# Four graph layers on one core: the leaky slope inside ScalarE's activation, another set-up, and new orders on every engine

## What is computed

```python
h = jnp.maximum(_layernorm(x, axis=-1), 0.0)
x = x + _L0_gnn_ref(h, ...)   # masked attention, 8 heads, projection, o + layernorm(o)
h = jnp.maximum(_layernorm(x, axis=-1), 0.0)
x = x + _L1_gnn_ref(h, ...)   # rel = adj.T * (h Wq.T)(h Wk.T).T / row norm; rel @ (h Wv.T)
h = jnp.maximum(_layernorm(x, axis=-1), 0.0)
x = x + _L2_gnn_ref(h, ...)   # graph attention, below
h = jnp.maximum(_layernorm(x, axis=-1), 0.0)
x = x + _L3_gnn_ref(h, ...)   # adj @ h @ weight + bias
```

```python
h = jnp.einsum('bnc,cf->bnf', x, W)
e = jax.nn.leaky_relu(s1[:, :, None] + s2[:, None, :], negative_slope=0.2)
e = e * mask[None, :, :]
att = jax.nn.softmax(e, axis=2)
return jax.nn.elu(jnp.einsum('bij,bjf->bif', att, h) + beta * h)
```

## Time and profile before

| | |
|---|---|
| median of 3 runs | 1473.15 us (1472.97 to 1476.63) |
| the profiled execution's own time | 1474.63 us |
| its span, first to last instruction | 1472.8 us |
| TensorE busy | 1438.2 us, 98% |
| VectorE busy | 1273.4 us, 86% |
| ScalarE busy | 1134.7 us, 77% |
| GpSimd busy | 748.4 us, 51% |

### The profile page before, as it was taken

One profiled execution on the slowest core, in us unless ns is written; L12 is line 12 of the kernel. 1 busy time (PEld: TensorE's weight loads), 2 busy tenths in 40 slices (PEclk: granted clock), 3 DMA queues, 4 the chain that ended last, 5 costly groups with the idle time before them and its releaser, 6 DMA issues.

```text
span 1472.8 us, 47814 instructions
## 1 busy us (share of the span) xinstructions
PE 1438.2 (98%) x16136; PEld 1370.3 (93%) x16136; DVE 1273.4 (86%) x5774; ACT 1134.7 (77%) x2884; POOL 748.4 (51%) x1107
## 2 busy tenths in 40 slices
PE   5999999999999999999999999999999999999996
PEld 5899999999999999999999999999999999999985
DVE  4889988988989889889889889889889889889885
ACT  4778878878877877877877778778778788788753
POOL 3455555555555555555555555555555555555452
PEclk9999999999999999999999999999999999999998
DMA  3000000100000000001001000000001001000000
GB/s 111 17 17 23 31 16 30 31 16 31 30 17 31 30 16 31 28 19 31 24 23 30 23 24 30 24 24 31 23 24 30 23 24 30 19 28 31 9 23 30
DMA packets 38113, 39.90 MB, mean 27 GB/s; under 512 B 2416, under 2 KB 37488, under 8 KB 37872
## 3 DMA queue, kind: packets, MB, share of 16 engines
q1 hardware_dynamic: 37872, 36.84, 7.9%
HBM read 20.05 MB, written 16.78 MB: 25 GB/s over the span
## 4 chain that ended last, share of the span: by engine, by line
PE 95%; DVE 1%; ACT 1%; issue 1%; POOL 0%; DMA 0%; SPq 0%; POOLq 0%; ACTq 0%; DVEq 0%
PE bank L314 34%; PE mid L314 15%; PE bank L349 6%; PE mid L358 5%; PE bank L520 5%; PE bank L370 4%; PE mid L458 4%; PE mid L374 4%; PE bank L330 4%; PE mid L488 4%; PE bank L417 4%; PE mid L330 2%; PE mid L349 2%; PE mid L493 1%; PE mid L527 1%
## 5 line engine op out<-in xcount | busy, mean ns | idle before, releaser
L546 ACT ACTIVATE probs<-masked,neg_max 128x128 f32<-128x128 f32 x1024 | 326.3, 395 | 6.3 <-DVE neg_max L716 6.3
L903 POOL TENSOR_TENSOR rstd<-var_eps,minus_half 128x2 f32<-128x2 f32 x320 | 240.9, 753 | 25.5
L716 DVE CUSTOM_DVE_ANT_0 masked<-mid,mask 128x128 f32<-128x128 f32 x1024 | 234.9, 286 | 6.9 <-issue 6.8
L915 POOL TENSOR_TENSOR xb<-x,b_proj_beta 128x512 f32<-128x512 f32 x64 | 81.9, 1279 | 233.9 <-DVE o_res L828 233.9
L901 POOL TENSOR_TENSOR var_eps<-mean_var,eps 128x2 f32<-128x2 f32 x320 | 63.5, 198 | 243.0 <-DVE mean_var L710 242.7
L706 DVE BATCH_NORM_STATS2 stats<-x 128x6 f32<-128x256 f32 x384 | 143.3, 415 | 0.1
L725 DVE TENSOR_SCALAR z<-x,mean_var,rstd 128x256 f32<-128x256 f32 x384 | 134.5, 405 | 7.1 <-POOL rstd L903 6.7
L946 POOL TENSOR_TENSOR h_t_lo<-h_t_full,h_t_hi 128x512 fp32r<-128x512 f32 x64 | 82.0, 1282 | 79.4 <-ACT h_t_hi L629 79.4
L349 PE MATMUL bank<-ident,probs 128*128 128x128 f32 x768 | 117.6, 276 | 4.9 <-ACT probs L546 4.9
L942 POOL TENSOR_TENSOR e_mask<-e_leaky,adj_sb 128x256 f32<-128x256 f32 x64 | 46.8, 731 | 116.2 <-DVE e_leaky L770 116.2
L370 PE MATMUL bank<-probs_t,v 128*32 128x128 f32 x2048 | 104.5, 276 | 0.3 <-issue 0.3
(11 more groups left out here) (156 smaller groups left out, 5725.8 us busy)
## 6 DMA issues: line engine op xcount, KB each, us to landing
x<-in_x SPq DMA_DIRECT2D x64, 256.0 KB, 2.7
out_x<-x SPq DMA_DIRECT2D x64, 256.0 KB, 2.1
w_qkv_sb<-in_w_qkv SPq DMA_DIRECT2D x1, 768.0 KB, 4.4
w_q_sb<-in_w_q SPq DMA_DIRECT2D x1, 256.0 KB, 4.4
w_k_sb<-in_w_k SPq DMA_DIRECT2D x1, 256.0 KB, 4.6
w_v_sb<-in_w_v_t SPq DMA_DIRECT2D x1, 256.0 KB, 5.8
w_proj_sb<-in_w_proj SPq DMA_DIRECT2D x1, 256.0 KB, 6.0
w_gat_x<-in_w_gat SPq DMA_DIRECT2D x1, 256.0 KB, 7.2
```

The costliest lines, as they stand in the source:

```text
L546: last = act.activation(probs[:, r, s], masked[:, r, s], ACT.Exp, scale=-1.0, bias=neg_max[:, r, s:s + 1])
L716: last = dve.tensor_tensor_reduce(out=masked[:, r, s], in0=mid[:, r, s * N:(s + 1) * N], in1=mask[:], scale=1.0, scalar=LARGE, op0=ALU.add ...
L903: pool.tensor_tensor(rstd[:, k], var_eps[:, k], minus_half[:], ALU.pow).then_inc(ln_rstd[k], 1)
```

## The change

**Leaky slope.** ScalarE reads s2 with the function Prelu and alpha 0.2 instead of Identity, with the same bias, and writes e_leaky itself. The tile e_sum, its semaphore and VectorE's pass are gone; GpSimd's e_mask now waits for two increments.

**Set-up.** w_qkv is rounded in three parts of 512 columns (q, k, v) on ScalarE and VectorE; both parts are issued ahead of VectorE's round 1, so the moments and z of pair 0 stand in front. TensorE's round 0 is only z0's transposes of pair 0; the fold stands behind them, ahead of round 1, and its two loads are issued behind CONSTS. ScalarE's copies of the fold come ahead of its round 2, its low part ahead of VectorE's round 3.

**Orders.** The order of the stages is another on all four engines, and so is the division into stages: k moves from on[0] to on[1] on TensorE, the transposes of probs 3 and the heads from on[1] to on[2], sum_sq to on[4], hw and s2 to on[5]. VectorE counts its stages one further (its last, x4, is on[8]), so `STREAMS` is 9; TensorE still uses on[0] to on[7]. The banks are assigned anew: z1, rel, y and the fold share bank 5, for instance. SP's loads and stores are counted to match.

```diff
-    STREAMS = 8
+    STREAMS = 9
...
             sp.dma_start(x0[:, 1], x_pairs[1]).then_inc(x_in[1], 16)
             for dst, src in CONSTS:
                 sp.dma_start(dst, src).then_inc(const_in, 16)
+            for dst, src in FOLD_CONSTS:
+                sp.dma_start(dst[:], src).then_inc(fold_in, 16)
...
+            def first_weights():
+                pe.wait_ge(fills_made, 3)
+                pe.wait_ge(w_lo_ready, 2)
...
-            run(pe, step, [(0, fold), (2, next_weights), (4, last_weights)])
+            run(pe, step, [(1, first_weights), (1, value_weights), (1, fold), (3, folded_weights),
+                          (2, next_weights), (5, last_weights)])
...
-            act.activation(w_qkv_p[0][:], w_qkv_sb[:], ACT.Copy).then_inc(w_hi_ready, 1)
+                for j in range(3):
+                    act.activation(w_qkv_p[0][:, :, j * D:(j + 1) * D], w_qkv_sb[:, :, j * D:(j + 1) * D], ACT.Copy)\
+                       .then_inc(w_hi_ready, 1)
...
-                    for b in range(2):
-                        act.activation(e_sum[:, b], s2_bank[:, b * N:(b + 1) * N], ACT.Identity, bias=hw[:, b, D:D + 1])\
-                           .then_inc(e_sum_ready, 1)
...
+                    for b in range(2):
+                        act.activation(e_leaky[:, b], s2_bank[:, b * N:(b + 1) * N], ACT.Prelu, bias=hw[:, b, D:D + 1], alpha=ALPHA)\
+                           .then_inc(e_leaky_ready, 1)
...
-            run(act, step, [(0, copy_fold)])
+            run(act, step, [(0, first_weights), (2, copy_fold)])
...
-                    dve.scalar_tensor_tensor(e_leaky[:], e_sum[:], ALPHA, e_sum[:], ALU.mult, ALU.max).then_inc(e_leaky_ready, 1)
...
-            run(dve, step, [(0, first_constants), (2, next_constants), (2, last_constants)])
+            run(dve, step, [(1, first_constants), (3, fold_low), (2, next_constants), (2, last_constants)])
...
-            run(pool, step, [(2, next_constants), (2, last_constants)])
+            run(pool, step, [(1, next_constants), (2, last_constants)])
```

## The result

The changed kernel took **1477.97 us** (median of 20 runs, 1474.88 to 1479.56), the kernel before beside it 1473.96 us (20 runs, 1472.97 to 1477.96): a ratio of **1.0021** (95% interval 1.0015 to 1.0028). By the ratio it is 3.1 us slower (the two medians lie 4.0 us apart). That is within the 0.3% that I called no change, and inside the range; but I had forecast a gain of 1 us, and the interval excludes one. The profiled execution took 1478.46 us with a span of 1476.6, 3.8 us more than the one of before.

The account below looks back on a forecast made before the run. TensorE, busy 98% and never waiting in the middle, was taken as the bound. Round +3.6, set-up -1.3 and drain -3.3 summed to -1.0 us: 1473.6 from the profiled 1474.63, 1472.2 against the median 1473.15; range 1466 to 1479.5.

Parts of the forecast that it names:

- no wait came up in front of scores: Saturated middle: scores waits for x2 to free its bank, with 1 us to spare, so TensorE never waits.
- one table load: ScalarE: Prelu shares the table set of Ln and Exp; the rival with table switches, about 1497 us, had chance 0.03.
- a slope that costs nothing: Leaky slope on ScalarE: Prelu pass 0.363 us, no gain in saturated rounds, about 0.5 us saved once in the drain.
- The round: TensorE's queue in the saturated middle: +0.06 us a round over some 60 rounds, +3.6 us (0 to +8.5).
- Joint (2): sum_sq on TensorE, moved from between u and probs 1's transposes to between k and hw: +0.05 to +0.10 us a round.
- All other joints: TensorE's other changes of matmul neighbours: fp32 transposes to fp32r almost free, into scores even, out of scores and heads nothing.
- The set-up: Start until TensorE is saturated, at q of pair 3: ahead by 1.3 us (-3 to +1).
- the landing of w_k: Set-up: w_k's load, issued behind CONSTS, lands at 12.6 us (11.5 to 13.5) and starts the fold.
- The drain: From q of pair 63 to the end: 84.1 us becomes 80.8, -3.3 us (-6 to 0).
- The 2 us at z2: Drain: z2 of pair 63 at 53.8 us, 2 us ahead, as x2 no longer stands behind three pieces of VectorE work.
- The wait of y for h1's copy: Drain: y of pair 59 shares a bank with z1 and waits for h1's copy, 0.2 us ahead of g.
- The rival "slower": The round costs 0.14 us more or above at the joints of sum_sq and heads with q: 1479.4 us, chance 0.12.

Follow-up runs that it names:

- the collision of round 4: Removed by moving VectorE's last constants behind pair 0's first maxima, against the changed kernel with fold loads and GpSimd's root moved earlier: 1473.61 us, ratio 0.9991.
- the loads alone: Changed kernel with the loads of w_q and w_k issued ahead of x of pair 1 again: 1476.82 us, ratio 1.0010.
- the drain with fillers: For the old order: kernel before plus 17 fp32 matmuls without a use in TensorE's drain gaps: 1470.28 us, ratio 0.9967.
- the kernel with the maxima freed: Changed kernel with GpSimd's root of pair 1 ahead of its constants and VectorE's last constants in round 4: 1478.24 us, ratio 1.0023.
- the slope alone: Kernel before with only the leaky slope moved to ScalarE's Prelu, VectorE's pass dropped: 1472.68 us, ratio 0.9990.
- The run with both chains freed: Changed kernel with w_q and w_k loaded earlier, GpSimd's root ahead of its constants, VectorE's last constants in round 4: 1475.67 us, ratio 0.9993.

## Why the prediction failed

**What held.** The middle is saturated and no wait came up in front of scores; one table load; a slope that costs nothing; z's transposes at 6.8 us.

**The round** was over-priced: +0.06 us forecast, +0.013 measured, so 0.75 us where I had put 3.6. Joint (2) itself is there:

```profile
612.27 0.50 PE L427 MATMUL bank<-ones,rel_sq 128*128 128x1 f32 x4
612.64 0.36 PE L320 MATMUL bank<-w_gat_hi,h_t_hi 128*128 128x258 f32 x1
612.84 0.28 PE L320 MATMUL bank<-w_gat_lo,h_t_hi 128*128 128x258 f32 x1
```

sum_sq still takes 0.37 us and hw's first step 0.20. Averaged over 50 rounds, from the start of one stage to that of the next, sum_sq and hw together take 0.084 us more, as (2) had it. All other joints, which I had counted at nothing, give 0.071 back: y_t takes 0.107 us less and rel_v 0.094 less, v 0.174 more, s2 0.079 more, and the rest is smaller.

**The set-up** is the step that failed: -1.3 us forecast, with +1 as the dear end, +4.1 measured. TensorE's part was nearly right: k at 18.03 us instead of 16.2, but scores at 22.83 where I had 22.3. It is the stretch behind, to the heads of pair 0, that failed: I gave it 8.4 us (22.3 to 30.7), and it took 11.8 (22.83 to 34.59). Three things were wrong in it. (a) I followed TensorE, and took VectorE's and GpSimd's queues as free ("to about 11.4 to 15.8 us, ahead of the inverse root of pair 1, which is needed at 22"). They ran until 16.6 us and the root behind them, and it is needed earlier, because VectorE's last constants stand behind the z that waits for it and ahead of the maxima. Freeing this chain and the loads together brought 3.2 us, and 5.1 with the collision of round 4 out of the way; the loads alone brought 1.6 by the ratios. (b) The prediction gives VectorE's last constants no time at all; two of their passes, 0.42 us each in the kernel before, where GpSimd is quiet, take 1.5 us here beside it. (c) I asked when the clock would rise (18.5 us, forecast 17.7) and not whether it would fall again: 1.8 to 2.2 us. The term that I had named as the risk, the landing of w_k, was 2.2 us late in the profiled execution (14.84 against 12.6) and 0.6 to 1.1 us in others, and it mattered only in second place: with the fold at 13.23 us q8 was 0.5 us earlier (149.18).

**The drain**: -3.3 us forecast, -1.1 measured. Here my walk compared like with unlike. I took the durations of the kernel before at half clock as properties of its order: "g at 39.7, as rel_v of pair 62 is out of its way (before 40.8)". At full clock the old order has its g at 39.7 as well. TensorE in the drain with fillers, z1, g, z2 and u of pair 63 in the old order (q of that pair at 1387.71):

```profile
1424.13 0.66 PE L330 MATMUL bank<-ident,z 128*128 128x128 f32 x4 [0.38 <-DVE z L736]
1427.39 0.38 PE L314 MATMUL bank<-h_t_hi,w_qk_hi 128*128 128x256 f32 x1 [0.33 <-POOL h_t_lo L957]
...
1442.59 0.66 PE L330 MATMUL mid<-ident,z 128*128 128x128 f32 x4 [0.62 <-DVE z L736]
...
1452.95 1.13 PE L497 MATMUL mid<-hw,att_t 128*128 128x256 f32 x4 [0.47 <-ACT att_t L669]
```

and z1, z2 and u in the new order (q at 1388.60):

```profile
1425.62 0.66 PE L336 MATMUL bank<-ident,z 128*128 128x128 f32 x4 [0.19 <-DVE z L760]
...
1443.51 0.66 PE L336 MATMUL bank<-ident,z 128*128 128x128 f32 x4 [0.62 <-DVE z L760]
...
1453.26 1.10 PE L544 MATMUL mid<-hw,att_t 128*128 128x256 f32 x4 [0.52 <-ACT att_t L640]
```

Counted from that q: z1, g, z2, u and the end at 36.4, 39.7, 54.9, 65.2 and 79.8 us in the old order, at 37.0, 40.4, 54.9, 64.7 and 79.1 in the new. The 2 us at z2 don't exist. z2 does follow rel_v of its pair by 5.2 us instead of 6.0, since x2 waits for less on VectorE; but rel_v comes 0.8 us later, as z1 is 0.6 us late and v1 stands ahead of rel. And I had put the clock's cost at 4 us before and 3 after; it is 4.3 (84.1 - 79.8) and 3.9 (83.0 - 79.1). So the drain gained 0.7 us by the order, by one profile of the old one with its own choice of fillers against three of the new, and 0.4 by the clock. The 0.4 says nothing of the change: eight profiles have the new order without fillers in the drain, and it took from 80.1 us (3.4 of them at half clock, the kernel with the maxima freed) to 85.7 us (20.5 at half clock, the one with the slope back on VectorE). The wait of y for h1's copy, 1.27 us idle where I had 0.2, is real but hardly on this path: in the changed kernel h1's low part, which g needs, is ready at 1433.79 us, and g starts at 1434.04.

The rival "slower" had the right sign and the wrong place: it sat in the round, which cost next to nothing. No case of mine rested on a set-up that gets longer by more than 1 us. That the time still fell inside the range is luck: the set-up was missed by 5.4 us and the drain by 2.2, and the round, priced 2.9 us too dear, took some of it back.

## What to carry to other kernels

When TensorE is saturated and an edit hardly changes the price of its own round (0.013 us here), it is won or lost at the ends, and there the queue to follow is not only TensorE's: walk every engine's queue of set-up work in order, with durations taken beside the neighbours that it will have. Ask of each end whether TensorE's pauses let the clock fall, and compare two orders at the same clock before crediting the order; a few idle matmuls, fewer than fit in the gap, are a cheap test of it, and here they were worth more than the change cost (4.4 us against 3.1). Where two chains end at the same place, an edit to either may show little and both together more than the sum (1.6 us, none, and 4.1 here): test them as a pair.

## What the runs showed of the hardware

VectorE's passes with two operands in SBUF slow down beside GpSimd's passes over 128x512: 1.47 to 1.51 us instead of 0.41, in all eight kernels in which they meet and at two different times, and 0.41 again as soon as GpSimd is quiet. The Trainium skill, "GPSIMD Engine Reference", opening table, names this contention of the shared SBUF interfaces for VectorE instructions with two SBUF inputs; the trace agrees and adds the factor of 3.6. z, with one tensor input, suffers as well: 1.97 us for its two halves beside GpSimd's xb, where the same two take 0.73 in the middle.

TensorE's clock falls in the ends of both kernels after short pauses: 0.6 and 1.2 us ahead of the fall at 1425.1 us in the kernel before, 2.2 and 0.7 us ahead of the one at 28.7 us in the changed kernel. The same queue doesn't fall at the same place every time: the old set-up kept 2.4 GHz at 26.9 us in one profile and fell there in another, that of the slope alone. 16 or 17 fp32 matmuls in the drain's pauses keep it at 2.4 GHz there, in one of the four profiles up to the last 0.6 us and in the others to the end. The Trainium skill, "TensorE: Matmul & The Clock Gate", Part 1, calls the half clock the default state, which activity lifts; the traces agree, and its price here is 3.9 us in 83. It also goes with most of the scatter: with fillers in the drain the five to eleven runs of a kernel lay within 1.2 to 1.8 us of each other, without them the runs of a kernel spread over 2.4 to 6.8 us. The run with both chains freed shows it best: four of its twelve, at a mean clock of 0.997, took 1471.1 to 1471.5 us, and seven at 0.992 to 0.994 took 1475.4 to 1476.3.
